# Six instead of eight token tiles normalised before the first head group, the first q weights prepared by three engines, and weight splits, statistics and a bias moved in the order

## The reference, cut to what matters

```python
x = x + tanh(g_xattn[0]) * L0_xattn(layernorm(x), ctx)   # 32 heads, 8 kv heads, biases bq, bkv, bo
x = x + tanh(g_ffn[0])   * L0_ffn(layernorm(x))          # 512 -> 2*1376 -> 512
x = x + tanh(g_xattn[1]) * L1_xattn(layernorm(x), ctx)   # keys: context + own tokens, rms-normed q and k
x = x + tanh(g_ffn[1])   * L1_ffn(layernorm(x))          # base + top-2 low-rank experts
```

## Time and profile before

| what | value |
|---|---|
| median of 3 runs | 1410.93 us (1410.56 to 1411.52) |
| profiled execution: its time / span | 1412.08 us / 1410.3 us |
| mean granted PE clock | 0.995 of full speed |
| busy PE / DVE / ACT / POOL | 1372.8 / 1050.7 / 803.8 / 487.4 us |
| HBM read | 60.97 MB, 45 GB/s over the span |

### The profile page before, as it was taken

How to read it: one execution, slowest core, us unless ns; L and a number is a source line. 1 busy time by engine, 2 the same in 40 slices (tenths; PEclk the granted TensorE clock), 3 DMA queues, 4 the chain that set the end, 5 groups by cost and what they waited for, 6 DMA issues and landing times.

```text
span 1410.3 us, 23780 instructions
## 1 busy us (share of the span) xinstructions
PE 1372.8 (97%) x7976; PEld 1193.5 (85%) x7976; DVE 1050.7 (75%) x2739; ACT 803.8 (57%) x2227; POOL 487.4 (35%) x615
## 2 busy tenths in 40 slices
PE   5999999999999998999999999999999999999998
PEld 5899999988888887888888888888888888888777
DVE  7777787778824447788787787787788778778875
ACT  6787787775402215565565555556556556556641
POOL 5865565555825512212212222122222221212220
PEclk9999999999999999999999999999999999999999
DMA  5221122221312300100101001001001001000001
GB/s 202 76 76 49 70 74 74 74 76 45 121 46 60 116 1 16 61 1 33 44 0 74 1 1 74 0 0 74 0 0 74 0 0 74 15 30 14 1 9 53
DMA packets 14942, 63.82 MB, mean 45 GB/s; under 512 B 1760, under 2 KB 1760, under 8 KB 10656
## 3 DMA queue, kind: packets, MB, share of 16 engines
q1 hardware_dynamic: 14880, 63.07, 12.7%
HBM read 60.97 MB, written 2.10 MB: 45 GB/s over the span
## 4 chain that ended last, share of the span: by engine, by line
PE 77%; DVE 12%; ACT 5%; POOL 3%; issue 2%; DMA 0%; ACTq 0%; SPq 0%; DVEq 0%; POOLq 0%
PE psum L58 23%; PE psum L60 22%; PE psum L59 22%; PE psum L1427 3%; ACT p L1294 2%; PE psum L1438 2%; DVE mx L1095 1%; DVE w1q_lo L1053 1%; PE psum L1459 1%; DVE VW_lo L362 1%; POOL w0q_lo L240 1%; DVE qT_lo L1090 1%; DVE pT_lo L1060 1%; PE psum L1422 1%; PE psum L111 1%
## 5 line engine op out<-in xcount | busy, mean ns | idle before, releaser
L1294 ACT ACTIVATE p<-psum,nb,rq 128x320 f32<-128x320 f32 x256 | 155.3, 614 | 156.6 <-DVE nb L1099 156.6
L1021 POOL TENSOR_TENSOR p<-p,rinv 128x640 f32<-128x640 f32 x64 | 80.2, 1254 | 203.5 <-DVE rinv L1105 203.5
L58 PE MATMUL psum<-w1q_hi,xnT_lo 128*128 128x512 f32 x288 | 119.6, 415 | 0.0
L60 PE MATMUL psum<-w1q_hi,xnT_hi 128*128 128x512 f32 x288 | 113.3, 394 | 0.0
L59 PE MATMUL psum<-w1q_lo,xnT_hi 128*128 128x512 f32 x288 | 112.7, 391 | 0.0
L1271 ACT ACTIVATE pT_hi<-psum 128x512 fp32r<-128x512 f32 x128 | 69.7, 596 | 69.0 <-PE psum L1427 69.0
L1060 DVE TENSOR_TENSOR pT_lo<-psum,pT_hi 128x512 fp32r<-128x512 f32 x128 | 85.2, 686 | 30.9 <-ACT pT_hi L1271 30.2
L1095 DVE TENSOR_REDUCE mx<-psum 128x2 f32<-128x640 f32 x128 | 104.5, 816 | 3.9 <-PE psum L60 3.9
L60 PE MATMUL psum<-w1o_hi,oT_hi 128*128 128x512 f32 x256 | 100.5, 393 | 0.0
L59 PE MATMUL psum<-w1o_lo,oT_hi 128*128 128x512 f32 x256 | 100.5, 393 | 0.0
L58 PE MATMUL psum<-w1o_hi,oT_lo 128*128 128x512 f32 x256 | 100.1, 391 | 0.0
(11 more groups left out here) (237 smaller groups left out, 4642.0 us busy)
## 6 DMA issues: line engine op xcount, KB each, us to landing
raw_q<-in_w0q SPq DMA_DIRECT2D x8, 1024.0 KB, 4.7
raw_o<-in_w0o SPq DMA_DIRECT2D x8, 1024.0 KB, 4.8
raw_q<-in_w1q SPq DMA_DIRECT2D x8, 1024.0 KB, 7.5
raw_o<-in_w1o SPq DMA_DIRECT2D x8, 1024.0 KB, 4.8
raw_kv<-in_w_gu SPq DMA_DIRECT2D x10, 512.0 KB, 3.5
raw_gu<-in_w_gu SPq DMA_DIRECT2D x10, 512.0 KB, 3.5
raw_kv<-in_w0kv SPq DMA_DIRECT2D x8, 515.0 KB, 3.4
raw_kv<-in_w1kv SPq DMA_DIRECT2D x8, 512.0 KB, 5.5
```

What stands on the lines that cost most here:

```text
L58: pe.matmul(out, w[1], m[0], start=start, stop=False)
L60: return pe.matmul(out, w[0], m[0], start=False, stop=stop)
L1021: pool.tensor_tensor(p, p, k.rinv[:, stat(j)].unsqueeze(2).to_broadcast([PART, 2, KEYS]), ALU.mult).then_inc(p_scaled_pool, 1)
L1294: last = act.activation(k.p1[:, tile, 2 * hp + hh, :], s_pair(j)[:, hh, :], ACT.Exp, bias=k.nb[:, i:i + 1], scale=k.rq[:, i:i + 1], accum_ ...
```

## The change

- Head of attention 0: only tiles 0 to 5 (`EARLY`) are normalised ahead of group 0. Tiles 6 and 7 (`LATE`) follow inside group 0: statistics at steps 2 and 3, normalising and transposing at steps 3 to 5, splits one step later, through the banks of the output product. Scores of tile s in group 0 wait for tile s alone. The first key preparation of the next group moves from step 3 to step 4 of group 0.
- Head q weights: the shift of pieces 2 and 3 goes from DVE to ACT, their low halves from DVE to POOL, between `pool_rstd` of tiles 1, 2 and 3. The low halves of `WK` now come behind those of `xnT`.
- All four pieces of the first o weights are split on POOL behind the last `pool_rstd`; their load is issued ahead of the last load of x.
- The bias add on POOL moves from group 0 to the last group.
- Attention 1: the last q piece is split by DVE in unit 0 of the next group, behind `cx_lo`; PE waits for each q piece at the matmuls that use it. The same piece in the tail waits behind `ln.dve_lo`, and `pe_base` of tile 0 waits piece by piece.
- First unit: `q_lo` of tile 0 ahead of the second `q_squares`; in unit 1 the query projection of tile 0 ahead of `turn` 2.
- Last group: the statistics of tiles 0 to 3 at the end of units 1 and 2 instead of within units 2 and 3.

```diff
+    EARLY, LATE = 6, {4: 6, 5: 7}
...
-    def steps_fills(s, nxt):
-        return OWN_PREP.get(s, []) + (NEXT_PREP.get(s, []) if nxt else [])
+    def steps_fills(s, nxt, first=False):
+        own, more = OWN_PREP.get(s, []), NEXT_PREP.get(s, []) if nxt else []
+        if first and s == 3:
+            return own
+        if first and s == 4:
+            return NEXT_PREP[3] + own + more
+        return own + more
+    def late_tile(s, first):
+        return LATE.get(s) if first else None
...
+        return o_bank[s % 2]
...
         for i in range(4):
+            if i == 3:
+                weights("o")
             sp.dma_start(k.x[:, 2 * i:2 * i + 2, :],
                          k.d["x"][i * 256:(i + 1) * 256, :].rearrange("(t p) c -> p t c", p=PART)).then_inc(in_x[i], 16)
-        weights("o")
         sp.dma_start(k.bo[:, :], k.d["bo"].to_broadcast([PART, HID])).then_inc(in_bo, 16)
...
+        def p_scale(g, t):
+            pool.wait_ge(p_rec, NT * g + t + 1)
+            p = by_head(k.p0[:, t % 4, :])
+            pool.tensor_tensor(p, p, spread(k.rinv0[:, t % 4, :]), ALU.mult).then_inc(p_ready, 1)
+        def first_body():
+            pool.wait_ge(q_in, 32)
+            p_scale(0, 0)
+            q_last_row(pool).then_inc(q_row_set, 1)
+            pool.wait_ge(kv_in, 32)
+            pool.wait_ge(prep_free, 2)
+            pool.tensor_tensor(k.bias[:, :], k.raw_kv[:, KVW:KVW + GH + 2], k.zeros[:, :], ALU.add).then_inc(bias_in, 1)
+            for i in range(CONV["kv"]):
+                hi_piece("kv", i)
+            p_scale(0, 1)
+            for i in range(CONV["kv"]):
+                lo_piece("kv", 1, i)
+            p_scale(0, 2)
+            ln.pool_rstd(pool, 0, LATE[4])
+            ln.pool_rstd(pool, 0, LATE[5])
+            for t in range(3, NT):
+                next_ready(1, t)
+                p_scale(0, t)
+                next_split(1, t)
...
+                p_scale(g, t)
...
-                if isinstance(g, int) and g == 0:
+                if not nxt:
+                    pool.wait_ge(x_done, NT * (NKV - 1))
                     pool.tensor_tensor(k.x[:, t, :], k.x[:, t, :], k.gbo[:, :], ALU.add).then_inc(bo_added, 1)
...
-        for t in range(NT):
+        for t in range(EARLY):
             ln.pool_rstd(pool, 0, t)
-            if t == 6:
-                pool.wait_ge(o_in, 16)
-                hi_piece("o", 0)
-                lo_piece("o", 0, 0)
-        for i in range(1, CONV["o"]):
+            if t in (1, 2):
+                lo_piece("q", 0, t + 1)
+        pool.wait_ge(o_in, 16)
+        for i in range(CONV["o"]):
             hi_piece("o", i)
             lo_piece("o", 0, i)
-        pool.wait_ge(gbo_done, 1)
-        pool.wait_ge(ln.xn, NT)
-        body(0, True)
+        first_body()
         with pool.Fori(1, NKV - 1) as g:
             body(g, True)
+        pool.wait_ge(gbo_done, 1)
...
-            if isinstance(g, int) and g == 0:
+            if isinstance(g, int) and g == 0 and t == 0:
+                dve.wait_ge(gates, 1)
+            if isinstance(g, int) and g == NKV - 1:
                 dve.wait_ge(bo_added, t + 1)
...
+                if late_tile(s + 2, first):
+                    stats(late_tile(s + 2, first))
+                if late_tile(s, first):
+                    ln.dve_lo(dve, 0, late_tile(s, first), late_bank(s))
...
-        for h in range(3):
+        for h in range(2):
             head_q_shift(h)
-        head_q_lo(0)
-        head_q_shift(3)
-        head_q_lo(1)
+        for h in range(2):
+            head_q_lo(h)
         prep(None, ("kv", 0))
         stats(0)
-        head_q_lo(2)
-        head_q_lo(3)
         stats(1)
         prep(None, ("kv", 1))
...
-        for t in range(NT):
-            if t + 1 < NT:
-                prep(None, HEAD_WK[t + 1])
-            if t + 3 < NT:
+        prep(None, HEAD_WK[1])
+        for t in range(EARLY):
+            if t + 3 < EARLY:
                 stats(t + 3)
             ln.dve_lo(dve, 0, t, head_bank(t))
+            prep(None, HEAD_WK[t + 2])
         prep(None, ("vw", 0, 0))
...
+                if late_tile(s - 1, first):
+                    ln.act_hi(act, 0, late_tile(s - 1, first), late_bank(s - 1))
+                for fill in steps_fills(s, nxt, first):
...
+                if late_tile(s + 1, first):
+                    ln.act_norm(act, 0, late_tile(s + 1, first))
...
-        for h in range(GH):
+        for h in range(2):
             head_q_hi(h)
-            if h == 1:
-                act.wait_ge(bias_in, 1)
-                prep(None, ("kv", 0))
+        act.wait_ge(bias_in, 1)
+        prep(None, ("kv", 0))
+        for h in range(2, GH):
+            act.activation(raw_q4[:, h, 0:HID - 1], raw_q4[:, h, 0:HID - 1], ACT.Identity,
+                           bias=k.q_last[:, h:h + 1]).then_inc(q_shifted, 1)
+            head_q_hi(h)
...
+        prep(None, HEAD_WK[1])
+        for t in range(EARLY):
+            if t + 1 < EARLY:
                 ln.act_norm(act, 0, t + 1)
             ln.act_hi(act, 0, t, head_bank(t))
+            prep(None, HEAD_WK[t + 2])
             if t == 3:
                 act.wait_ge(in_small, 32)
                 act.activation(k.gate[:, :], k.gate_raw[:, :], ACT.Tanh).then_inc(gates, 1)
+        prep(None, ("vw", 0, 0))
+        body(0, True)
...
         act.activation(k.gbo[:, :], k.bo[:, :], ACT.Copy, scale=k.gate[:, 0:1]).then_inc(gbo_done, 1)
...
+                    if first:
+                        pe.wait_ge(ln.split, s + 1)
...
+                    if late_tile(s - 1, first):
+                        pe.wait_ge(ln.split, late_tile(s - 1, first) + 1)
...
+                if late_tile(s, first):
+                    pe.wait_ge(x_done, s - 3)
+                    ln.pe_turn(pe, 0, late_tile(s, first), late_bank(s))
...
+        prep(None, HEAD_WK[1], 0)
+        for t in range(EARLY):
             ln.pe_turn(pe, 0, t, head_bank(t))
+            prep(None, HEAD_WK[t + 2], 0)
...
-        pe.wait_ge(ln.split, NT)
         body(0, True, True)
...
+                if prev and b == 0:
+                    w_lo("q", g, CONV["q"] - 1)
...
-                if not nxt and b >= 2:
-                    ln.dve_stats(dve, 3, 2 * b - 4)
-                    ln.dve_stats(dve, 3, 2 * b - 3)
...
+                if not prev:
+                    q_lo(n, b, 0, True)
                 q_squares(n, 1)
-                q_lo(n, b, 0, not prev)
+                if prev:
+                    q_lo(n, b, 0)
...
-                for c in conv[5:6]:
-                    w_lo(*c)
                 t_lo(n, b, 0)
                 row_max(n, 3)
                 t_lo(n, b, 1)
+                if not nxt and b in (1, 2):
+                    dve.wait_ge(x_added, 2 * u + 2)
+                    ln.dve_stats(dve, 3, 2 * b - 2)
+                    ln.dve_stats(dve, 3, 2 * b - 1)
...
             ln.dve_lo(dve, *ln_tiles(u)[1], ln_bank(BATCH - 1, 1))
+            w_lo("q", NKV, CONV["q"] - 1)
...
             for c in range(CH):
+                if b == 0 and tile == 0:
+                    pe.wait_ge(q_wlo, CONV["q"] * g + c + 1)
...
                 else:
+                    pe.wait_ge(kv_split, n + 1)
+                    q_proj(g, b, 0)
...
-                if b == 0:
-                    pe.wait_ge(q_wlo, CONV["q"] * (g + 1))
                 if b % 2 == 0 and prev:
                     pe.wait_ge(cx_split, 2 * g + b // 2 + 1)
-                else:
+                elif not (first and b == 1):
                     pe.wait_ge(kv_split, n + 1)
-                q_proj(n, b, 0, not prev)
+                if not (first and b == 1):
+                    q_proj(g, b, 0, not prev)
...
-        if s == 0:
-            pe.wait_ge(self.free["q"], self.conv["q"] * (NKV + 1))
...
+            if s == 0:
+                pe.wait_ge(self.free["q"], self.conv["q"] * NKV + c + 1)
```

More of the change, by code:

```diff
@@ L173, in place, with late_bank @@
         return at, k.bank[slot % 3]
-    def steps_fills(s, nxt):
-        return OWN_PREP.get(s, []) + (NEXT_PREP.get(s, []) if nxt else [])
+    def steps_fills(s, nxt, first=False):
[7 more added lines that the diff above has]
+        return LATE.get(s) if first else None
+    def late_bank(s):
+        return o_bank[s % 2]
     def wk_view(w, c, hp):
@@ L278, in split_kv @@
                 lo_piece("kv", g, i)
+        def p_scale(g, t):
[21 more added lines that the diff above has]
+                next_split(1, t)
         def body(g, nxt):
             if nxt:
-                first = isinstance(g, int) and g == 0
-                split_kv(g + 1, 2 if first else HEAD + FILLS * (g - 1) + ORDER.index(("kv", 1)) + 1)
+                split_kv(g + 1, HEAD + FILLS * (g - 1) + ORDER.index(("kv", 1)) + 1)
             for t in range(NT):
@@ L286, in body @@
                     next_ready(g + 1, t)
-                pool.wait_ge(p_rec, NT * g + t + 1)
-                p = by_head(k.p0[:, t % 4, :])
```

(35 more changed lines are left out.)

## The result

The changed kernel takes 1400.82 us in the median of 6 runs (1399.45 to 1401.85), the kernel before beside it 1411.22 (1409.12 to 1411.70). The ratio is 0.9927, with a 95% interval from 0.9914 to 0.9940: 0.73% faster. The range on record holds it; the predicted time was 1397.3, 3.5 us less, and the gain was put at 13.6 where the two medians of this set differ by 10.4. The profiled execution took 1399.78 us, with a span of 1397.9.

What follows compares the result with a forecast made beforehand. PE was taken as the bound, busy 1372.8 of 1410.3 us, so gains come only from its waits and low clock. Terms summed to 13.6 us off the profiled 1412.1, giving 1398.5, or 1397.3 at the median; range 1392 to 1403.5.

Steps and rivals of the forecast that it cites:

- head: scores start: Head of attention 0: first scores start at 28.4 us against 34.8 at full clock, POOL setting the pace; gain 6.4 us.
- group 0: Attention 0, group 0: the two late tiles' eight transposes come back as PE work, costing 1.0 us.
- bias adds, last group: Last group: a 1.30 us add on POOL with 0.80 idle ahead makes its last p later, costing 0.5 us.
- first units: First unit of attention 1: query projection fills PE's waits, but PE then waits for k_raw; gain 2.1, bounds 0 and 5.7.
- moved q piece: Starts of groups 1 to 7, attention 1: v_lo waits go, 7/8 of 6.3 us; gain 5.5, bounds 6.3 and 1.0.
- last group: Last group: moved statistics and q piece remove 2.6 us of waits, against 0.8 and 0.7 of new cost; gain 1.1.
- group 0 stalls on the late tiles: Rival, group 0: DVE waits for ACT's copy with maxima and row sums queued behind; costs 3.0 us, 1400.3; chance 0.09.
- The key preparation moved to step 4 costs nothing: Group 0: same PE work, needed 5 steps later; if its cover went, it would cost DVE's 0.4 us.
- The wait of 0.73 for the last q piece: Group 0: POOL loses eight bias adds, gains two pool_rstd; PE's wait was left standing, between 0 and 1.5 us.
- the clock falls once or twice more: Rival: half clock in head (about 1.4 us) or attention 1's unit 1 (3.4); 1398.7 to 1402.1 us; chance 0.30.
- the q piece costs the same in its new place: Rival, attention 1: the moved piece's split takes as long as before, costing 4.5 us, 1401.8; chance 0.12.
- slower: Rival: waits ahead of k_raw drop the clock at every group start in attention 1, costing 23.9 us, 1421; chance 0.04.

Runs made afterwards that it cites:

- late_hi_first: The changed kernel with ScalarE copying the late tile (xnT_hi) in group 0 ahead of the next tile's normalisation and q shift: 1399.85 us, ratio 0.9916.
- eight_in_head: The changed kernel with all eight tiles normalised in the head: 1403.33 us, ratio 0.9946.
- bias_back: The changed kernel with the eight bias adds back on GpSimd in group 0, none in the last group: 1401.69 us, ratio 0.9932.
- first_units_back: The changed kernel with the second unit's q projection back behind p times v and q_squares ahead of q_lo: 1400.93 us, ratio 0.9931.
- head_alone: The kernel before with only the changed attention 0, attention 1 and last layer as before: 1408.54 us, ratio 0.9986.
- q_piece_back: The changed kernel with attention 1's fourth q piece split again at the end of the unit before: 1407.85 us, ratio 0.9974.
- last_piece_first: The changed kernel with the tail's q piece split first on DVE, ahead of dve_iota, dve_top and dve_lo: 1400.08 us, ratio 0.9919.

## Why the prediction held, and where not

By its own steps, against the pair of profiled executions (1412.08 and 1399.78, 12.3 us):

| step | predicted | measured |
|---|---|---|
| head: scores start | 6.4 (28.4) | 5.9 (28.92) |
| group 0 | -1.0 | -3.0 |
| bias adds, last group | -0.5 | -0.3 |
| first units | +2.1 | +2.2 |
| moved q piece | +5.5 | +6.6 |
| last group | +1.1 | +1.0 |
| sum | 13.6 | 12.4 |

**Head and group 0 is the step that failed**: 2.9 for 5.4. Half a microsecond is the head's: POOL's chain of six `pool_rstd`, two q and two o pieces ended at 28.0 instead of 27.3, for 0.4 since three of the six took 1.49 and not 1.35, and the fill behind it took 0.8 instead of 1.1. Two are group 0's, where I charged only the transposes' 1.0. The table's -1.99 is against a group 0 that had 1.0 of half clock in it, so it is -3.0 at full clock: 1.0 for the transposes, 0.93 at 37.90, 0.67 at 48.20, and 0.4 that no wait holds. The 0.67 is the rival "group 0 stalls on the late tiles", which I gave 0.09; it came beside the forecast, and `late_hi_first` took it back with 0.3 of the 0.4.

The 0.93 is the sentence "The key preparation moved to step 4 costs nothing". Its cover went, and that cost 0.93 and not the 0.4 that I had put for that case. This is the kernel before at the same place:

```profile
41.26 0.28 PE L58 MATMUL psum<-ctxT_hi,w_kv_lo 128*128 128x256 f32 x1
...
43.16 0.43 DVE L398 TENSOR_TENSOR pT_lo<-psum,pT_hi 128x256 fp32r<-128x256 f32 x1
...
44.09 0.38 PE L600 MATMUL psum<-ident,p 128*128 128x128 f32 x2
```

From 41.26 to 42.67 PE makes the twelve matmuls of the key preparation, and comes to the transposes at 44.09, when `pT_lo` is done. Meanwhile ACT and DVE copy and subtract VW (1.2 and 1.39 us a step) ahead of `pT_lo`. That chain is as long in all three kernels: from the start of PE's last product of VW ahead of it (40.48, 34.65 and 39.65 in the kernel before, the changed one and `eight_in_head`) to that of `pT_lo` (43.16, 37.33 and 42.34) it takes 2.68 us or 2.69. Without the 1.41 us of key preparation between, PE waits 0.93 in the changed kernel and 0.94 in `eight_in_head`, which has the preparation at step 4 too. The half clock of the kernel before isn't what hid the chain: it was over at 35.84, well ahead of this place, and the chain takes as long in the kernel that had no half clock. No run puts the preparation alone back to step 3.

**The wait of 0.73 for the last q piece** was left standing, and it does stand (0.74). That it came out as taken is luck: the adds that left POOL (2.1 by `bias_back`) and the earlier PE seem to cancel, which no run tried apart.

**First units**: the size was right for the pair, the reason only in half. Between `first_units_back` and the changed kernel it is 1.1 without a fall; the other 1.2 is the half-clock stretch, which is 3.4 us in the trace of `head_alone` and 6.83 in that of the kernel before, though nothing around it is edited. What made it shorter stays open. I wrote 0 to 5.7 as bounds, and had not thought that this stretch could have another length.

**Moved q piece**: the mechanism is as told, what was mis-sized is the term 7/8 of 6.3. The seven waits at starts of groups were 5.70 us, as the eighth was the short one, and what goes is the distance of the starts of PE around them, 6.57, not the idle of the waits' rows. The price of 1.32 in the old place and 0.68 in the new is shown in all eight pieces: `q_piece_back` has them at 1.31 and 1.32 again. The Trainium skill (GPSIMD Engine Reference, Specifications) names the contention for instructions with two SBUF inputs; the traces agree, 839 ns against 683 in the mean, though no run moves POOL's work away and leaves the piece where it was.

**Last group**: the sum is right, its parts are not, and that is luck. The waits of 0.66, 0.84 and 1.06 went, and one of 0.37 with them: 2.9 for 2.6. The waits of 0.44 and 0.36 that are left were there before (0.35 each), so the statistics cost 0.1 and not 0.8. `pe_base` paid 1.64, not 0.7.

**The median against the pair.** The forecast started from a profiled execution with two half-clock stretches and ended in one with none. The rival "the clock falls once or twice more" holds in part of the executions. Behind the 2.05 us for `k_raw` the clock falls in four of the variants' traces (`q_piece_back`, `last_piece_first`, `late_hi_first`, `bias_back`) and not in four others with the same wait; its price is 1.5 us (513.95 for 512.46), where I had 3.4. In the head it falls in two traces with six tiles there, where I had 1.4, and no price is to be seen. The median of 1400.82 lies 1.0 above the profiled execution. The first of these falls would explain it, as the runs from 1400.77 up have a mean clock of 0.999 or 0.998, but they have no trace. The kernel before has better executions too: beside the experiments, 8 of 38 had a mean clock of 0.998 or 0.999 and took 1408.94 to 1410.27. Between the fastest of both kernels lie 9.5 us (1408.94 and 1399.44), not 12.3. The Trainium skill (TensorE: Matmul & The Clock Gate, Part 1) says that the moment at which a busy engine comes to its full clock moves from run to run. No run here shows that moment apart; what they show is that one kernel has a mean clock of 1.000, 0.999 or 0.998. What sets it in a single run stays open.

The rivals "the q piece costs the same in its new place" and "slower" fell: 683 ns, and no third low stretch at a group's start.

## What to carry to other kernels

Work of the busiest engine that moves to another step costs nothing only if it covered nothing: read how long the other engines' chain beneath it takes and where the busiest engine would stand without it (here 1.41 us of matmuls over a chain that then held it 0.93). Price a removed wait by the distance of the starts around it, not by the idle in its row. Where an engine in list order waits for a copy by another, put that copy ahead of work that nobody waits for; here that, one piece at the tail and one scaling gave 2.3 us more for three moved lines.

## What the runs showed of the hardware

A wait of 0.82 us cost PE 0.95, 0.13 of it after the release; seven such waits, 5.70 us by their rows, cost 6.57. A subtraction of 128x512 on DVE took 1.31 or 1.32 us in each of eight places, each time with POOL scaling p at its start, and 0.69 or less in its new place. The same wait of 2.05 us for `k_raw` was followed by 3.4 us at 1.2 GHz in four traces and by none in four others, and such a stretch cost 1.2 to 1.7 us. A stretch of the same length in the head, where PE waits for POOL anyway, cost nothing to be seen in two traces. The half-clock stretch behind the waits of 1.8 and 1.09 us was 6.83 us in the trace of the kernel before and 3.4 in those of `head_alone` and `first_units_back`; the cause of that is not shown.
